# Quantised activations turned by a transposing DMA instead of TensorE, and gate matmuls ahead of up matmuls, in a fused convolution and quantised FFN kernel

## The chip, the cores and the metric

One core of one Trainium2 chip. The metric is the device time of one launch in microseconds; lower is better. Times of the kernel before: three runs, 221.1, 221.6 and 222.94 us, median 221.6. One further execution was profiled.

## The reference

The input x is 64 x 32 x 512 (batch, head, position), float32. What is computed, with the parameters' set-up left out:

```
kernel = S4D kernel of 32 heads, 512 taps (exp, sin, cos of 64 modes a head)
u      = x masked to each batch row's length
y      = (causal convolution of u with kernel + D * u), masked again
beta   = mean |y| over the 512 positions
q      = clip(round(y * sqrt(7) / (beta + 1e-5)), -8, 7)          # int4 values
gate   = q @ ternary(w_gate).T,  up = q @ ternary(w_up).T          # 512 -> 1376
inter  = up * relu(gate)^2       (with the scales of q and of the weights)
inter  = clip(round(inter * 127 / (max|inter| + 1e-5)), -128, 127) # int8 values
out    = x + inter @ ternary(w_down).T (with scales)               # 1376 -> 512
```

## The kernel before, in words

The 64 x 32 rows of 512 are cut into T = 16 tiles of 128 rows (two heads by 64 batch rows). A prologue of some 42 us loads and quantises the three weight matrices and makes the convolution's taps, which go to a buffer in DRAM, `k_back`. Then the loop over tiles runs, software-pipelined over three tiles and written out by hand: each engine has its own `body(m, j, p, k)`, called for k = 0 to 16 (SyncE to 17), with m = k and p = k % 2, and engines meet at semaphores alone. Each engine works its list in order, so a wait holds all that is listed behind it. The work of one tile n:

- **SyncE** loads x into `x_in` (two halves), and from `k_back` the Toeplitz matrix `toep` of the tile's two heads (512 KB), both by `load_ahead(m + 3, ...)`, and later x again as `x_res`. Nearly every large transfer is issued from this queue. The order in body m is: the transposing DMA of tile m - 1's `inter_q` into `it_int` (L365, waits for `inter_quant`), the store of tile m - 2's output (L369), `load_ahead(m + 3)` (L294, L316), `x_res` of tile m (L374). `load_ahead` is called for k < 13 only.
- **TensorE** turns x (`xt`, L465), into `tr_act_ps`; multiplies by `toep` (`conv`, L475), 16 records a tile; turns the rounded y (`qt`, L488: four 128 x 128 transposes into `tr_dve_ps`); makes gate and up in three chunks of 416, 512 and 448 columns (`products`, L562 and L564, four matmuls of each to a chunk, gate and up alternating); and multiplies by the down weights (`down`, L600, 11 matmuls). Body m holds: products 0 and 1 of tile m, xt(m + 2), products 2, down(m - 1), qt(m + 1), conv(m + 2). Gate and up have two PSUM banks each, taken in turn, so chunk 2 uses those of chunk 0 and waits for `relu_done` and `inter_ready` of chunk 0.
- **ScalarE** copies x's transpose (L652), sums |y| (`y_sum`, L657), rounds y (`y_round`, L661), and makes relu (L693) and square (L696) of each gate chunk. In body m: chunk 0, y_sum(m + 1), chunk 1, y_round(m + 1), chunk 2, the copy of x(m + 2).
- **VectorE** masks conv's result into `y` (L960), makes the scales (`y_scale`, L966 to L970), clips q into `q_t` (`q_copy`, L974), makes `inter` from up and the squared relu (L1034) and its maxima (L1038), quantises it (L1089), casts `it_int` to `i_t` (L1058), and adds the residual (L1105). In body m, from 2 on: gated(0), the cast of tile m - 1, y_scale(m + 1), gated(1), gated(2), q_copy(m + 1), the maximum and scales, the quantise of tile m, o_sb of tile m - 1, y_mask(m + 2).

`y_round` adds the float 1.5 * 2^23, so that the low 16 bits of the float32 `y_r` hold the integer; `y_low` is that half seen as bfloat16, and the transpose moves its bits unchanged. `q_copy` reads them from PSUM as int16 and clips to -8 to 7.

Of the kernel before, what the change touches and what calls it, by code (L numbers as in the profile page):

```python
# [20 lines left out]
P = 128  # L21
# [17 lines left out]
def adaln_ffn(nc, x, length, log_dt, C, log_A_real, A_imag, Dskip,  # L39
# [21 lines left out]
    with ExitStack() as ctx:  # L61
# [85 lines left out]
        y = sb("y", [P, L])  # L147
        y_r = sb("y_r", [P, L])
        ysum = [sb(f"ysum{p}", [P, 1]) for p in range(2)]
# [18 lines left out]

        y_low = y_r[:].bitcast(BF16)[:, ::2]
        by_re, by_im = (inter[:, i * HG * JB:(i + 1) * HG * JB].rearrange("p (c k) -> p c k", c=2) for i in range(2))  # L170
# [47 lines left out]
        q_copied = sem("q_copied")  # L218
        gu_done = sem("gu_done")
        relu_done = sem("relu_done")  # L220
# [63 lines left out]
        def _(sp):  # L284
# [74 lines left out]
            def body(m, j, p, k):  # L359
                if k == 1:  # L360
                    turn_down(0)
                if 1 <= k < T:
                    sp.wait_ge(inter_quant, m)
                    wait(sp, it_dve_copied, m - 1)
                    sp.dma_start_transpose(it_int[:], inter_q[:]).then_inc(it_loaded, 16)  # L365
                if k >= 2:
                    sp.wait_ge(out_ready, m - 1)
                    for half in range(2):
                        sp.dma_start(in_dram(out, m - 2, half), o_sb[p][half_rows(half), :]).then_inc(stored[p], 16)  # L369
                if k < T - 3:  # L370
                    load_ahead(m + 3, 1 - p)
                if k is None or k < T:
                    for half in range(2):
                        sp.dma_start(x_res[p][half_rows(half), :], in_dram(x, m, half)).then_inc(res_loaded[p], 16)  # L374
                if k == 0:
                    turn_down(1)
# [62 lines left out]
        def _(pe):  # L439
# [40 lines left out]
            def qt(n):  # L480
# [6 lines left out]
                for i in range(KB):  # L487
                    mm = pe.transpose(q_bank(n)[:, i * P // 2:(i + 1) * P // 2].bitcast(BF16),  # L488
                                      y_low[:, i * P:(i + 1) * P], ident_bf[:])
                mm.then_inc(q_turned, 1)  # L490
# [61 lines left out]
            def products(m, p, c, k):  # L552
                c0, cn = CH[c]
                bank = (NC * p + c) % 2
                pe.wait_ge(q_copied, m + 1)
                if k == 0:
                    wait(pe, w_dve_copied, copies_before(c, COPY_DVE))
                    pe.wait_ge(w_act_copied, copies_before(c, COPY_ACT))
                wait(pe, relu_done, NC * m + c - 1)
                wait(pe, inter_ready, NC * m + c - 1)  # L560
                for i in range(KB):
                    pe.matmul(gate_ps[bank][:, 0:cn], q_t[p][:, i, :], gate_t[:, i, c0:c0 + cn],  # L562
                              start=(i == 0), stop=(i == KB - 1))
                    mm = pe.matmul(up_ps[bank][:, 0:cn], q_t[p][:, i, :], up_t[:, i, c0:c0 + cn],  # L564
                                   start=(i == 0), stop=(i == KB - 1))
                mm.then_inc(gu_done, 1)

# [36 lines left out]
            def body(m, j, p, k):  # L604
# [13 lines left out]
                if k >= 2:  # L618
                    down(m, k)
                if k < T - 1:  # L620
                    qt(m + 1)
                if k < T - 2:
# [8 lines left out]
        def _(act):  # L631
# [22 lines left out]
            def y_sum(n, p):  # L654
                act.wait_ge(y_masked, n + 1)
                wait(act, q_turned, n)
                nc.scalar.activation(y_r[:], y[:], ACT.Abs, accum_out=ysum[p][:]).then_inc(y_summed, 1)  # L657

            def y_round(n):
                act.wait_ge(yscale_ready, n + 1)  # L660
                nc.scalar.activation(y_r[:], y[:], ACT.Identity, bias=round_col[:],  # L661
                                     scale=yscale[:]).then_inc(y_rounded, 1)

# [23 lines left out]
            def body(m, j, p, k):  # L687
                def relu_square(c):
                    cn = CH[c][1]
                    bank = (NC * p + c) % 2  # L690
                    act.wait_ge(gu_done, NC * m + c + 1)
                    wait(act, inter_ready, NC * m + c - 1)
# [35 lines left out]
        def _(dve):  # L728
# [243 lines left out]
            def q_copy(n, p):  # L972
                dve.wait_ge(q_turned, n + 1)
                v.tensor_scalar(q_t[p][:].rearrange("p k t -> p (k t)"), q_bank(n)[:, 0:L // 2].bitcast(I16),  # L974
                                -8.0, 7.0, ALU.max, ALU.min).then_inc(q_copied, 1)

# [42 lines left out]
            def body(m, j, p, k):  # L1019
# [9 lines left out]
                def gated(c):  # L1029

                    c0, cn = CH[c]
                    bank = (NC * p + c) % 2
                    dve.wait_ge(g2_ready, NC * m + c + 1)
                    v.scalar_tensor_tensor(out=inter[:, c0:c0 + cn], in0=up_ps[bank][:, 0:cn],  # L1034
                                           scalar=gu_scale[p][:, 1:2], in1=g2[bank][:, 0:cn],
# [40 lines left out]
                if k < T:  # L1076
                    step(gated(2))
                if 1 <= k < T - 1:
                    q_copy(m + 1, 1 - p)
                if k is None or k < T:  # L1080
# [3 lines left out]
                    step(v.tensor_scalar(gam127[:], gamma[:], EPS, 1.0 / 127.0, ALU.add, ALU.mult))  # L1084
                    step(v.reciprocal(iscale[:], gam127[:]))
                    if k != T - 1:
                        if k >= 1:
# [56 lines left out]
```

## Time and profile before

| | before |
|---|---|
| runs, us | 221.1, 221.6, 222.94 (median 221.6) |
| profiled execution, us | 221.94 |
| its span, us | 220.1 |
| granted TensorE clock, mean | 0.997 |
| TensorE matmul busy | 182.1 us, 83% |
| VectorE busy | 168.0 us, 76% |
| ScalarE busy | 115.2 us, 52% |
| GpSimd busy | 9.6 us, 4% |
| DMA queue of SyncE | 63.3% of 16 engines' time, 36.40 MB |

The span is what the profile's clock covers, from the first to the last instruction; the execution's own time has 1.8 us more around it. Busy time is the sum of what an engine's instructions take; TensorE's records overlap, because a matmul's record runs on while the next has started, so the distance from start to start tells what one costs. A name such as `g` or `ysum` in a row is a tile with its buffer number left out. In a row of the timeline, what stands in brackets at the end is the idle time before it and what ended it.

### The profile page before, as it was taken

How to read it: one execution, taken by the hardware profiler on the slowest of the kernel's cores; microseconds unless marked ns; L12 is line 12 of the kernel's file. 1: busy time of each engine (PE TensorE's matmuls, PEld its weight loads, DVE VectorE, ACT ScalarE, POOL GpSimd, SP SyncE). 2: the span in 40 equal slices, each digit the busy share in tenths (PEclk: the TensorE clock that was granted, in tenths of full speed). 3: DMA queues.
4: the chain of work that ended last, by engine and by line, in shares of the span. 5: the costliest groups of instructions: out<-in, count | busy, mean ns of one | idle time of the engine just before them, and what ended most of it. 6: DMA issues, size and time to landing. Idle time of an engine off the chain costs nothing.

```text
span 220.1 us, 3405 instructions
## 1 busy us (share of the span) xinstructions
PE 182.1 (83%) x1139; PEld 94.2 (43%) x1139; DVE 168.0 (76%) x457; ACT 115.2 (52%) x182; POOL 9.6 (4%) x27
## 2 busy tenths in 40 slices
PE   1010499699859899999999999999999999997882
PEld 1010296454324345455454545444545545443340
DVE  6999677769839687787878787878678787878671
ACT  2365976599812528273554546382827364553610
POOL 4043500000000000000000000000000000000000
PEclk9999999999999999999999999999999999999998
DMA  3999049992994929485856657584949475251613
GB/s 77 386 378 284 5 108 339 300 264 55 209 224 89 231 84 230 107 232 101 223 113 195 136 169 164 143 208 111 224 111 244 89 227 111 60 121 43 150 30 76
DMA packets 43824, 36.61 MB, mean 166 GB/s; under 512 B 30240, under 2 KB 30304, under 8 KB 43808
## 3 DMA queue, kind: packets, MB, share of 16 engines
q1 hardware_dynamic: 43488, 36.40, 63.3%
q8 instruction: 9, 0.15, 0.3%
q0 software_dynamic: 256, 0.00, 0.1%
q14 instruction: 7, 0.06, 0.1%
q10 hardware_dynamic: 64, 0.00, 0.0%
HBM read 25.27 MB, written 4.28 MB: 134 GB/s over the span
## 4 chain that ended last, share of the span: by engine, by line
PE 54%; DVE 3%; issue 3%; DMA 2%; ACT 1%; DVEq 0%
PE down_ps L600 14%; PE gate_ps L562 13%; PE up_ps L564 12%; PE conv_ps L475 12%; PE tr_act_ps L465 2%; DMA it_int<-inter_q 2%; PE tr_dve_ps L488 1%; PE conv_ps L519 1%; DVE inter L1034 1%; ACT g L693 1%; ACT g L696 1%; DVE i_t L1058 0%; DVE inter_q L1089 0%; ACT i_t L709 0%; DVE o_sb L1105 0%
## 5 line engine op out<-in xcount | busy, mean ns | idle before, releaser
L562 PE MATMUL gate_ps<-gate_t,q_t 128*128 128x416 bf16 (+2 forms) x192 | 68.6, 357 | 3.3 <-DVE q_t L974 2.1
L564 PE MATMUL up_ps<-up_t,q_t 128*128 128x416 bf16 (+2 forms) x192 | 68.5, 357 | 0.0
L693 ACT ACTIVATE g<-gate_ps,gu_scale 128x416 f32<-128x416 f32 (+2 forms) x48 | 30.3, 631 | 65.5 <-issue 50.4
L1034 DVE SCALAR_TENSOR_TENSOR inter<-up_ps,gu_scale,g 128x416 f32<-128x416 f32 (+2 forms) x48 | 33.2, 692 | 24.1 <-ACT g L696 24.1
L600 PE MATMUL down_ps<-down_t,i_t 128*128 128x512 bf16 (+1 forms) x176 | 40.7, 379 | 3.5 <-DVE down_t L955 1.9
L475 PE MATMUL conv_ps<-toep,x_t 128*64 128x512 f32 (+3 forms) x256 | 38.0, 439 | 1.6 <-ACT x_t L652 1.5
L1038 DVE TENSOR_REDUCE imax<-inter 128x1 f32<-128x416 f32 (+2 forms) x48 | 30.3, 631 | 1.7
L562 PEld LDWEIGHTS gate_ps<-gate_t,q_t 128*128 128x128 bf16 x192 | 18.7, 97 | 25.2 <-issue 7.3
L696 ACT ACTIVATE g<-g 128x416 f32<-128x416 f32 (+2 forms) x48 | 28.1, 585 | 1.5
L600 PEld LDWEIGHTS down_ps<-down_t,i_t 128*128 128x128 bf16 (+1 forms) x176 | 16.9, 98 | 23.9 <-DVE i_t L1058 4.0
L475 PEld LDWEIGHTS conv_ps<-toep,x_t 128*64 128x64 f32 x256 | 17.0, 136 | 21.2 <-issue 15.6
L564 PEld LDWEIGHTS up_ps<-up_t,q_t 128*128 128x128 bf16 x192 | 18.8, 98 | 15.0
L457 PE MATMUL down_ps<-wsum,averaging 128*128 128x1 f32 x12 | 2.6, 324 | 19.2 <-ACT int_gate L634 10.4
L661 ACT ACTIVATE y_r<-y,round_col,yscale 128x512 f32<-128x512 f32 x16 | 13.0, 813 | 10.3 <-DVE yscale L970 10.1
L1089 DVE TENSOR_SCALAR inter_q<-inter,iscale 128x1376 int16<-128x1376 f32 x15 | 14.0, 936 | 0.5
L1105 DVE SCALAR_TENSOR_TENSOR o_sb<-down_ps,oscale,x_res 128x512 f32<-128x512 f32 x16 | 11.9, 746 | 2.6 <-PE down_ps L600 2.6
L1058 DVE CAST i_t<-it_int 128x1408 bf16<-128x1408 int16 x15 | 7.8, 520 | 6.5 <-DMA it_int<-inter_q 6.5
L960 DVE SCALAR_TENSOR_TENSOR y<-steps,lens,conv_ps 128x512 f32<-128x512 f32 x16 | 11.8, 740 | 1.1 <-PE conv_ps L475 1.1
L657 ACT ACTIVATE y_r<-y 128x512 f32<-128x512 f32 x16 | 9.8, 614 | 2.4 <-DVE y L960 2.4
L457 PEld LDWEIGHTS down_ps<-wsum,averaging 128*128 128x128 f32 x12 | 2.4, 279 | 19.9 <-ACT int_gate L634 10.5
L465 PE MATMUL tr_act_ps<-ident,x_in 128*128 128x128 f32 x64 | 9.7, 275 | 0.0
L652 ACT COPY x_t<-tr_act_ps 128x512 f32<-128x512 f32 x16 | 9.1, 568 | 1.0 <-PE tr_act_ps L465 1.0
(169 smaller groups left out, 165.6 us busy)
## 6 DMA issues: line engine op xcount, KB each, us to landing
toep<-k_back SPq DMA_DIRECT2D x16, 512.0 KB, 4.9
x_in<-in_x_dram SPq DMA_DIRECT2D x32, 128.0 KB, 3.1
x_res<-in_x_dram SPq DMA_DIRECT2D x32, 128.0 KB, 4.0
out_dram<-o_sb SPq DMA_DIRECT2D x32, 128.0 KB, 2.6
raw_down<-in_L_ffn_w_down_dram SPq DMA_DIRECT2D x2, 1376.0 KB, 8.8
raw_gate<-in_L_ffn_w_gate_dram SPq DMA_DIRECT2D x1, 1536.0 KB, 7.0
raw_up<-in_L_ffn_w_up_dram SPq DMA_DIRECT2D x1, 1536.0 KB, 14.2
raw_gate<-in_L_ffn_w_gate_dram SPq DMA_DIRECT2D x1, 1024.0 KB, 9.3
```

The lines of the kernel that those rows point to most:

```text
L465: mm = pe.transpose(tr_act_ps[:, i * P:(i + 1) * P], x_in[p][:, i * P:(i + 1) * P], ident[:])
L475: mm = pe.matmul(conv_ps[half * B:(half + 1) * B, 0:L - i * P], x_t[:, i, half * B:(half + 1) * B], toep[p][:, half, i * P:L], start=(i == ...
L562: pe.matmul(gate_ps[bank][:, 0:cn], q_t[p][:, i, :], gate_t[:, i, c0:c0 + cn], start=(i == 0), stop=(i == KB - 1))
L564: mm = pe.matmul(up_ps[bank][:, 0:cn], q_t[p][:, i, :], up_t[:, i, c0:c0 + cn], start=(i == 0), stop=(i == KB - 1))
L600: mm = pe.matmul(down_ps[:], i_t[0:r, c, :], down_t[0:r, c, :], start=(c == 0), stop=(c == IB - 1))
L661: nc.scalar.activation(y_r[:], y[:], ACT.Identity, bias=round_col[:], scale=yscale[:]).then_inc(y_rounded, 1)
L693: nc.scalar.activation(g2[bank][:, 0:cn], gate_ps[bank][:, 0:cn], ACT.Relu, scale=gu_scale[p][:, 0:1]).then_inc(relu_done, 1)
L696: nc.scalar.activation(g2[bank][:, 0:cn], g2[bank][:, 0:cn], ACT.Square).then_inc(g2_ready, 1)
L1034: v.scalar_tensor_tensor(out=inter[:, c0:c0 + cn], in0=up_ps[bank][:, 0:cn], scalar=gu_scale[p][:, 1:2], in1=g2[bank][:, 0:cn], op0=ALU.mu ...
L1038: return v.tensor_reduce(imax[:, c:c + 1], inter[:, c0:c0 + cn], AX.X, ALU.max, apply_absolute_value=True)
L1089: v.tensor_scalar(inter_q[:, 0:I], inter[:], iscale[:], None, ALU.mult).then_inc(inter_quant, 1)
L1105: v.scalar_tensor_tensor(out=o_sb[1 - p][:], in0=down_ps[:], scalar=oscale[1 - p][:], in1=x_res[1 - p][:], op0=ALU.mult, op1=ALU.add).then ...
```

## The change

From tile 2 on, q is no longer turned on TensorE. `y_round` writes int16 directly into `y_i` (the sum of |y| now writes into a bfloat16 tile `y_abs`), SyncE issues a transposing DMA from `y_i` to `q_int` in bodies 1 to 14, between `load_ahead` and `x_res`, and `q_copy` reads `q_int` from SBUF. On VectorE `q_copy` moves from ahead of the maximum to between the reciprocal `iscale` and the quantise. Tiles 0 and 1 are still turned on TensorE. In `products` the four gate matmuls of a chunk come first, with a semaphore of their own (`gate_done`), then the wait for `inter_ready`, then the four up matmuls (`up_done`); relu waits for `gate_done` alone and the product on VectorE for `up_done` too.

```diff
@@ -145,7 +145,9 @@
         toep = [sb(f"toep{p}", [P, 2, L]) for p in range(2)]
         x_t = sb("x_t", [P, KB, P])
         y = sb("y", [P, L])
-        y_r = sb("y_r", [P, L])
+        y_abs = sb("y_abs", [P, L], BF16)
+        y_i = sb("y_i", [P, L], I16)
+        q_int = sb("q_int", [P, KB, P], I16)
         ysum = [sb(f"ysum{p}", [P, 1]) for p in range(2)]
         ybe = sb("ybe", [P, 1])
         yinv = sb("yinv", [P, 1])
...
@@ -369,6 +372,10 @@
                         sp.dma_start(in_dram(out, m - 2, half), o_sb[p][half_rows(half), :]).then_inc(stored[p], 16)
                 if k < T - 3:
                     load_ahead(m + 3, 1 - p)
+                if 1 <= k < T - 1:
+                    sp.wait_ge(y_rounded, m + 2)
+                    sp.wait_ge(q_copied, m + 1)
+                    sp.dma_start_transpose(q_int[:], y_i[:]).then_inc(q_loaded, 16)
                 if k is None or k < T:
                     for half in range(2):
                         sp.dma_start(x_res[p][half_rows(half), :], in_dram(x, m, half)).then_inc(res_loaded[p], 16)
...
@@ -486,7 +493,7 @@
                 wait(pe, q_copied, n)
                 for i in range(KB):
                     mm = pe.transpose(q_bank(n)[:, i * P // 2:(i + 1) * P // 2].bitcast(BF16),
-                                      y_low[:, i * P:(i + 1) * P], ident_bf[:])
+                                      y_i[:, i * P:(i + 1) * P].bitcast(BF16), ident_bf[:])
                 mm.then_inc(q_turned, 1)
 
             def copied(k):
...
@@ -557,13 +564,15 @@
                     wait(pe, w_dve_copied, copies_before(c, COPY_DVE))
                     pe.wait_ge(w_act_copied, copies_before(c, COPY_ACT))
                 wait(pe, relu_done, NC * m + c - 1)
+                for i in range(KB):
+                    mm = pe.matmul(gate_ps[bank][:, 0:cn], q_t[p][:, i, :], gate_t[:, i, c0:c0 + cn],
+                                   start=(i == 0), stop=(i == KB - 1))
+                mm.then_inc(gate_done, 1)
                 wait(pe, inter_ready, NC * m + c - 1)
                 for i in range(KB):
-                    pe.matmul(gate_ps[bank][:, 0:cn], q_t[p][:, i, :], gate_t[:, i, c0:c0 + cn],
-                              start=(i == 0), stop=(i == KB - 1))
                     mm = pe.matmul(up_ps[bank][:, 0:cn], q_t[p][:, i, :], up_t[:, i, c0:c0 + cn],
                                    start=(i == 0), stop=(i == KB - 1))
-                mm.then_inc(gu_done, 1)
+                mm.then_inc(up_done, 1)
 
             def turn_last():
 
...
@@ -617,8 +626,8 @@
                     turn_last()
                 if k >= 2:
                     down(m, k)
-                if k < T - 1:
-                    qt(m + 1)
+                if k == 0:
+                    qt(1)
                 if k < T - 2:
                     conv(m + 2, j + 1, p)
                 if k == 1:
...
@@ -653,13 +662,15 @@
 
             def y_sum(n, p):
                 act.wait_ge(y_masked, n + 1)
-                wait(act, q_turned, n)
-                nc.scalar.activation(y_r[:], y[:], ACT.Abs, accum_out=ysum[p][:]).then_inc(y_summed, 1)
+                nc.scalar.activation(y_abs[:], y[:], ACT.Abs, accum_out=ysum[p][:]).then_inc(y_summed, 1)
 
             def y_round(n):
                 act.wait_ge(yscale_ready, n + 1)
-                nc.scalar.activation(y_r[:], y[:], ACT.Identity, bias=round_col[:],
-                                     scale=yscale[:]).then_inc(y_rounded, 1)
+                if 1 <= n <= 2:
+                    act.wait_ge(q_turned, n)
+                if n >= 3:
+                    act.wait_ge(q_loaded, 16 * (n - 2))
+                nc.scalar.activation(y_i[:], y[:], ACT.Copy, scale=yscale[:]).then_inc(y_rounded, 1)
 
             for g in range(2):
                 act.dma_start(ldt_in[:, g:g + 1],
...
@@ -688,7 +699,7 @@
                 def relu_square(c):
                     cn = CH[c][1]
                     bank = (NC * p + c) % 2
-                    act.wait_ge(gu_done, NC * m + c + 1)
+                    act.wait_ge(gate_done, NC * m + c + 1)
                     wait(act, inter_ready, NC * m + c - 1)
                     nc.scalar.activation(g2[bank][:, 0:cn], gate_ps[bank][:, 0:cn], ACT.Relu,
                                          scale=gu_scale[p][:, 0:1]).then_inc(relu_done, 1)
...
@@ -970,9 +981,14 @@
                 v.tensor_scalar(yscale[:], yinv[:], SQRT7, None, ALU.mult).then_inc(yscale_ready, 1)
 
             def q_copy(n, p):
-                dve.wait_ge(q_turned, n + 1)
-                v.tensor_scalar(q_t[p][:].rearrange("p k t -> p (k t)"), q_bank(n)[:, 0:L // 2].bitcast(I16),
-                                -8.0, 7.0, ALU.max, ALU.min).then_inc(q_copied, 1)
+                dst = q_t[p][:].rearrange("p k t -> p (k t)")
+                if n < 2:
+                    dve.wait_ge(q_turned, n + 1)
+                    src = q_bank(n)[:, 0:L // 2].bitcast(I16)
+                else:
+                    dve.wait_ge(q_loaded, 16 * (n - 1))
+                    src = q_int[:].rearrange("p k t -> p (k t)")
+                v.tensor_scalar(dst, src, -8.0, 7.0, ALU.max, ALU.min).then_inc(q_copied, 1)
 
             def k_copy(i):
 
...
@@ -1031,6 +1047,7 @@
                     c0, cn = CH[c]
                     bank = (NC * p + c) % 2
                     dve.wait_ge(g2_ready, NC * m + c + 1)
+                    dve.wait_ge(up_done, NC * m + c + 1)
                     v.scalar_tensor_tensor(out=inter[:, c0:c0 + cn], in0=up_ps[bank][:, 0:cn],
                                            scalar=gu_scale[p][:, 1:2], in1=g2[bank][:, 0:cn],
                                            op0=ALU.mult, op1=ALU.mult).then_inc(inter_ready, 1)
...
@@ -1075,14 +1092,14 @@
                     weight_round(2, 1)
                 if k < T:
                     step(gated(2))
-                if 1 <= k < T - 1:
-                    q_copy(m + 1, 1 - p)
                 if k is None or k < T:
 
                     step(v.tensor_reduce(gamma[:], imax[:], AX.X, ALU.max))
                     v.tensor_scalar(oscale[p][:], gamma[:], wscale_dn[:], None, ALU.mult)
                     step(v.tensor_scalar(gam127[:], gamma[:], EPS, 1.0 / 127.0, ALU.add, ALU.mult))
                     step(v.reciprocal(iscale[:], gam127[:]))
+                    if 1 <= k < T - 1:
+                        q_copy(m + 1, 1 - p)
                     if k != T - 1:
                         if k >= 1:
                             dve.wait_ge(it_loaded, 16 * m)
```

## Rows read from the trace of the kernel before

**Rows 1.** Waits of 85 to 187 us: total, times, longest.
```profile
PEld gate_ps L562 <- issue: 3.9, 20, 0.2
```

**Rows 2.** Timeline of TensorE over one tile: start, us, instruction, [idle before].
```profile
124.40 0.60 PE L465 MATMUL tr_act_ps<-ident,x_in 128*128 128x128 f32 x4
125.01 0.35 PE L562 MATMUL gate_ps<-gate_t,q_t 128*128 128x448 bf16 x1
...
126.52 2.54 PE L600 MATMUL down_ps<-down_t,i_t 128*128 128x512 bf16 x11
128.90 0.39 PE L488 MATMUL tr_dve_ps<-ident_bf,y_r 128*128 128x128 bf16 x4
129.22 2.37 PE L475 MATMUL conv_ps<-toep,x_t 128*64 128x512 f32 x16
131.53 0.35 PE L562 MATMUL gate_ps<-gate_t,q_t 128*128 128x416 bf16 x1
```

**Rows 3.** Timeline of TensorE in the last tile but one.
```profile
196.88 0.35 PE L562 MATMUL gate_ps<-gate_t,q_t 128*128 128x448 bf16 x1 [0.45 <-DVE inter L1034]
```

**Rows 4.** Timeline of TensorE in the first tile.
```profile
48.60 0.64 PE L465 MATMUL tr_act_ps<-ident,x_in 128*128 128x128 f32 x4
49.07 0.35 PE L562 MATMUL gate_ps<-gate_t,q_t 128*128 128x448 bf16 x1
```

**Rows 5.** Timeline of VectorE and ScalarE over the same tile as rows 2.
```profile
124.22 0.65 DVE L1034 SCALAR_TENSOR_TENSOR inter<-up_ps,gu_scale,g 128x416 f32<-128x416 f32 x1 [1.26 <-ACT g L696]
...
125.41 0.52 DVE L1058 CAST i_t<-it_int 128x1408 bf16<-128x1408 int16 x1
...
126.60 0.81 ACT L661 ACTIVATE y_r<-y,round_col,yscale 128x512 f32<-128x512 f32 x1 [0.63 <-DVE yscale L970]
...
127.32 0.61 ACT L693 ACTIVATE g<-gate_ps,gu_scale 128x448 f32<-128x448 f32 x1
...
129.94 0.42 DVE L974 TENSOR_SCALAR q_t<-tr_dve_ps 128x512 bf16<-128x512 int16 x1
...
130.97 0.94 DVE L1089 TENSOR_SCALAR inter_q<-inter,iscale 128x1376 int16<-128x1376 f32 x1
```

**Rows 6.** Timeline of SyncE's queue over the same tile.
```profile
121.67 1.45 SPq L365 DMA_TRANSPOSE it_int<-inter_q  x1
123.17 1.39 SPq L369 DMA_DIRECT2D out_dram<-o_sb  x2
...
125.89 0.69 SPq L316 DMA_DIRECT2D toep<-k_back  x1
...
131.94 1.42 SPq L365 DMA_TRANSPOSE it_int<-inter_q  x1
```

**Rows 7.** The line of toep in 85 to 187 us: durations in ns, landings.
```profile
L316 SPq DMA_DIRECT2D toep<-k_back x10: 589/592/1535, 85.0 to 177.2; - x10
...
DMA to landing us min/median/max: 4.4/5.0/5.7
```

**Rows 8.** DMA issues of the whole span: us from issue to landing (median).
```profile
it_int<-inter_q SPq DMA_TRANSPOSE x15, 3.6
...
int_gate<-int_down SPq DMA_TRANSPOSE x2, 5.4
```

**Rows 9.** Stretches of one tile; last two columns: DMA share, GB/s.
```profile
121.50:122.50 1.00, 1.00 (x7) 0.54 (x6) 1.00 (x3) 0.00 (x0) 0.00 (x0) 1.00 0.00 0
123.00:124.50 1.50, 1.50 (x9) 0.73 (x7) 0.28 (x1) 1.47 (x3) 0.00 (x0) 1.00 1.11 212
...
127.50:129.50 2.00, 2.00 (x14) 1.00 (x13) 1.33 (x3) 1.48 (x3) 0.00 (x0) 1.00 0.94 297
```

**Rows 10.** SyncE's queue around the first changed tiles.
```profile
63.36 0.59 SPq L316 DMA_DIRECT2D toep<-k_back  x1
...
70.03 1.41 SPq L365 DMA_TRANSPOSE it_int<-inter_q  x1
```

**Rows 11.** The line of the it_int transpose in 85 to 187 us.
```profile
L365 SPq DMA_TRANSPOSE it_int<-inter_q x10: 1300/1411/1449, 90.9 to 183.3; - x10
```

More of the change, by code:

```diff
@@ L166, in adaln_ffn @@
         o_sb = [sb(f"o_sb{p}", [P, L]) for p in range(2)]
-        y_low = y_r[:].bitcast(BF16)[:, ::2]
         by_re, by_im = (inter[:, i * HG * JB:(i + 1) * HG * JB].rearrange("p (c k) -> p c k", c=2) for i in range(2))
@@ L218, in adaln_ffn @@
         q_copied = sem("q_copied")
-        gu_done = sem("gu_done")
+        q_loaded = sem("q_loaded")
+        gate_done = sem("gate_done")
+        up_done = sem("up_done")
         relu_done = sem("relu_done")
```

## The prediction

> **What bounds the kernel now.** I read the waits first, then the timeline of one tile on each engine, then the landings of the transfers. In the steady stretch TensorE has no wait of its own in the view of waits; all that it shows at a chunk's first matmul is a weight load that comes 0.2 us late, 20 times for ten tiles [rows 1]. The timeline of a tile shows why the period is what it is: the first gate matmul of the next tile starts at 131.53, and the queue of SyncE repeats after 131.94 - 121.67 = 10.27 us [rows 2, 6]. Two items of that are not products. The four transposes of q hold TensorE from 128.90 to 129.22, 0.32 us. The gap from the input transposes to chunk 2 is 125.01 - 124.40 = 0.61 us, where the first tile, with nothing to wait for, needs 49.07 - 48.60 = 0.47 [rows 2, 4]. The other 0.14 is a wait for VectorE: chunk 2 shares its banks with chunk 0, and the product that frees them ends at 124.22 + 0.65 = 124.87 [rows 5]; where no input transpose lies between, the same wait shows in full, 0.45 us [rows 3]. So TensorE is the bound, and 0.46 us of its tile could go.
>
> A second ring is nearly as long, and the reader must see it before believing that gain. It goes from the transpose of inter_q (issued 121.67) to its landing 3.6 us later [rows 6, 8], the cast into i_t at 125.41, the y scale, y_round at 126.60, the relu of chunk 2 behind it at 127.32, the product, the maximum, q_copy at 129.94, the quantise at 130.97, and the next issue at 131.94 [rows 5, 6]. The landing is at 125.27 and the cast at 125.41, so the slack is at most 0.14 us: this ring needs 10.13.
>
> The third view is the queue of DMAs. SyncE issues, in this order and without pause, the transpose (A), the output 1.50 us later, x_in, toep at A + 4.22, x_res [rows 6]. The engines are idle before A's packets arrive, then run at 212 GB/s and a share of 1.11 without change from 123.0 to 124.5, though the output was issued at 123.17, and the rest follows (297 GB/s at 127.5 to 129.5) [rows 9]. What is issued on this queue is served in order, then. toep lands a median 5.0 us (4.4 to 5.7) after its issue [rows 7], at A + 9.2, only about 1 us before the next A.
>
> **The change part by part.** Off TensorE: from tile 2 on 0.32 us of q transposes go. Whether the 0.09 or so between the last of them and conv (four at about 0.06 make 0.23) is theirs or conv's own start can't be told; 0.23 to 0.32 goes. The 0.14 of chunk 2 goes as well: its gate matmuls now wait only for relu(0), and the four of them cover the wait for the product, which now guards the up matmuls alone. TensorE would need 10.27 - 0.14 - (0.23 to 0.32) = 9.81 to 9.90 us. The regrouped order costs nothing else: each matmul had its own weight load before and has it still. relu(0) is released four matmuls (some 0.7 us) earlier, but the ring above starts at the cast, which waits for the transfer; that gain is hidden.
>
> ScalarE: y_round writes int16 and has no bias tile. Rows give 0.81 us for it now; nothing shows the new form, which I put at 0.61 (the relu of 448 columns) to 0.81, no change taken. Its new wait for the q of the tile before, and the lost wait of y_sum for q_turned, are long satisfied.
>
> VectorE: q_copy reads int16 from SBUF in place of PSUM, 0.42 us now. The cast of 1408 columns takes 0.52 [rows 5], so 512 columns take between 512/1408 of that, 0.19, and 0.42; I take 0.3, of which 0.25 passes before the quantise can start. What matters is its new place: ahead of the quantise, on an engine that works in order. **Its wait for q_loaded now holds the quantise, its output transpose, the o_sb product and y_mask, and through them everything that SyncE issues next.**
>
> SyncE: the new issue stands behind toep. It waits for y_rounded, which comes at 126.60 + 0.81 = 127.41, A + 5.74; x_res behind it has a whole tile of time, and the wait for q_copied is old. So it is issued some 1.2 us later than the queue would allow, and what then counts is when the transfer lands.
>
> **The landing of q.** The trace has no 512-column transpose. The one of 1408 columns lands in 3.6 us, the one of 2816 in 5.4 [rows 8]: 1.8 us per 1408 columns, so 0.65 us of transfer for 512 and 1.8 before and after it. On an empty queue it would land 2.45 us after its issue, at A + 8.2. But the queue isn't empty: 512 KB of toep are ahead of it and land at A + 9.2, and in order it can't land before them. So q lands at A + 4.22 + 5.0 + 0.65 = A + 9.87 (9.27 to 10.57 with the ends of toep). Then 0.05 until VectorE starts, 0.25 of q_copy, and 130.97 to 131.94, 0.97, from the quantise to the next issue: the ring is **9.87 + 0.05 + 0.25 + 0.97 = 11.14 us**, against 10.27. Everything in it is measured from A, so a longer tile doesn't give the queue time to drain; TensorE waits some 1.2 us per tile at q_copied instead of bounding it.
>
> The Trainium skill bears on this from two sides. "DMA: Bandwidth & Descriptors", Queues, rings and completion order, says that each DMA engine takes descriptors in ring order and that the completion lands after everything earlier on that engine; the rates above agree. The same page, Anatomy of one DMA, fits 2.0 us plus bytes over 436 GB/s for a transfer (on GpSimd's path): an estimate of 2.3 us for these 128 KB, by which q would land at A + 8.0 and the first rival below would hold; for toep the same fit gives 3.2 us, where the trace has 5.0, and the measurement decides.
>
> **The sum.** The issues of the inter_q transpose from tile 2's body (70.03) to tile 13's (183.28) are 11 periods, 113.25 us [rows 10, 11]; at 11.14 they take 122.5, +9.3. The first q by DMA (body 1) lands at 63.36 + 5.0 + 0.65 = 69.0, and 1.27 later, at 70.3, comes the issue that was at 70.03 [rows 10]: +0.3. From body 13 on no toep is loaded, so q is in time there: two periods at about 10.06 (next paragraph), -0.4, and the 0.45 us wait in rows 3 partly gone, -0.2. Together +9.0 on the profiled execution's 221.94 (span 220.1), which stands 0.34 above the median of 221.6: 230.6 us on the scale of the median.
>
> **Rivals.** *Hidden transfer, faster.* If q isn't held by toep (served beside it, or toep lands sooner once x_res is issued after it), it lands before the maxima are done, at about A + 8.9, and the second ring bounds: 10.13 less 0.12 to 0.17 for the shorter q_copy, less 0 to 0.2 if y_round shrinks, 9.8 to 10.0 us. 13 periods save 3.5 to 6, the last tiles 0.5: 216 to 218, say 217.5. For it: the empty-queue price of 2.45 us. Against it: the order of service in rows 9. Chance 0.17. *Short tail of toep.* toep lands in 4.4 always, since nothing reads HBM behind it: ring 10.54, +2.6 for 11 periods, +0.3 - 0.6: 224. Chance 0.13. *Transfer dearer.* If the transpose can't start until the last engine has finished toep and then pays part of its start again (1.8 us less what overlaps, say 0.6), the ring is 11.74: +15.9 - 0.3, 237. Chance 0.08. *The regrouping undoes itself* (up matmuls wait for the product and the 0.14 stays): less than 2 us, inside the other cases; 0.02 for that with a hidden transfer, no change.
>
> **How the numbers follow.** Forecast 0.60: 230.6 us, with 227 to 234 for it alone. One per cent is about what a measurement of this kernel can tell from no change. Faster by over 1%: the hidden transfer, 0.17. Within 1% (219.4 to 223.8): the undoing and the low part of the short tail, 0.08. Slower: 0.75. The range reaches from within the short tail to the dearer transfer, 222 to 237.
>
> **What would show it.** Right: the q transpose issued about 5.8 us after the one of inter_q and landing at least 3.5 us after its own issue, behind toep; idle time of VectorE at q_copy put down to that DMA; TensorE idle 1 us or more at L562's place; ScalarE's first relu of a tile starting while the up matmuls of chunk 0 still run. Period 11.1 with toep, about 10.0 without. Wrong: a landing within 2.5 us of the issue, a period under 10.1, and TensorE without a gap. The weakest step is that a transpose queued behind toep adds its 0.65 us and no more to toep's last landing; and it would also be wrong if toep's 5.0 us hangs on what is behind it.

## The result, and the profile after

The changed kernel is slower: 228.14 us median against 222.03 us of the kernel before in the same session, ratio 1.0285 with an interval of 1.0217 to 1.0353. The profiled execution took 230.12 us, the longest of its runs; the others lie between 227.49 and 228.23. Ratios leave out an execution more than 1.5% longer than the fastest of its kernel, and the profiled executions of two kernels below (with a dash in the table) are such ones, so that of their rows only the landing of q is read. A ratio isn't exactly the quotient of the medians.

The page of the changed kernel, its span, busy time of the engines and the chain that ended last by engine:

```profile
span 228.3 us, 3326 instructions
...
PE 179.1 (78%) x1083; PEld 90.8 (40%) x1083; DVE 167.3 (73%) x457; ACT 114.5 (50%) x182; POOL 9.4 (4%) x27
...
DMA 31%; DVE 13%; PE 7%; ACT 4%; SPq 2%; issue 2%; DVEq 0%
```

TensorE has less to do than before (179.1 us of busy time against 182.1), and the chain has left it: in the kernel before TensorE's part of the chain was 54% of the span, now it is 7%, and 31% is DMA, half of that each for the transpose of inter_q and the one of y. TensorE's clock isn't the cause: from 70 us to 192 us the granted clock is 1.00, and in the run with the transposing DMA alone, as slow as this one, its mean is 1.000. The waits say who stands still for them (total, times, longest):

```profile
DVE i_t L1075 <- DMA it_int<-inter_q: 15.8, 15, 4.3
...
DVE q_t L991 <- DMA q_int<-y_i: 12.3, 9, 2.1
PE gate_ps L568 <- DVE q_t L991: 11.9, 11, 2.3
```

VectorE waits at q_copy, for the new transfer; TensorE waits at the first gate matmul of a tile, for q_copy. One tile, where the kernel before has [rows 5, 6] (line numbers have moved: L368 is the transpose of inter_q, L319 toep, L378 the new transpose, L991 q_copy, L1106 the quantise):

```profile
125.02 1.40 SPq L368 DMA_TRANSPOSE it_int<-inter_q  x1
...
128.58 0.53 DVE L1075 CAST i_t<-it_int 128x1408 bf16<-128x1408 int16 x1 [0.87 <-DMA it_int<-inter_q]
...
129.24 0.59 SPq L319 DMA_DIRECT2D toep<-k_back  x1
...
129.78 0.72 ACT L673 ACTIVATE y_i<-y,yscale 128x512 int16<-128x512 f32 x1 [1.48 <-DVE yscale L981]
130.41 0.61 ACT L704 ACTIVATE g<-gate_ps,gu_scale 128x448 f32<-128x448 f32 x1
...
130.53 1.21 SPq L378 DMA_TRANSPOSE q_int<-y_i  x1
...
133.54 0.16 DVE L1100 RECIPROCAL iscale<-gam 128x1 f32<-128x1 f32 x1
...
134.97 0.29 DVE L991 TENSOR_SCALAR q_t<-q_int 128x512 bf16<-128x512 int16 x1 [1.26 <-DMA q_int<-y_i]
135.17 0.93 DVE L1106 TENSOR_SCALAR inter_q<-inter,iscale 128x1376 int16<-128x1376 f32 x1
...
135.31 0.88 PE L568 MATMUL gate_ps<-gate_t,q_t 128*128 128x416 bf16 x4 [0.78 <-DVE q_t L991]
...
136.13 1.43 SPq L368 DMA_TRANSPOSE it_int<-inter_q  x1
```

Read it from A = 125.02. toep is issued at A + 4.22 as before. y_round ends at 130.50 and q's transpose is issued at once, at A + 5.51. The scale that the quantise needs is ready at 133.70. The quantise starts at 135.17 all the same, because q_copy stands ahead of it and waits 1.26 us for q. The next issue is at 136.13: 11.11 us after A, where the tile in [rows 6] took 10.27. Landings in us after the issue, medians from 60 to 212 us, beside [rows 7, 8]:

```profile
toep<-k_back SPq DMA_DIRECT2D x12, 512.0 KB, 4.6
...
it_int<-inter_q SPq DMA_TRANSPOSE x15, 3.5
q_int<-y_i SPq DMA_TRANSPOSE x14, 4.2
```

In this tile toep lands 4.9 us after its issue, at 134.1. q lands 4.34 us after its own issue, as the chain has it:

```profile
130.53 4.34 DMA q_int<-y_i
```

That is 134.87, some 0.7 us behind toep, though q was issued 3.6 us before toep's landing. In the bodies without a toep load the same transpose lands in 2.5 us:

```profile
q_int<-y_i SPq DMA_TRANSPOSE x1, 2.5
```

The issues of the inter_q transpose from tile 2's body to tile 13's, beside [rows 10, 11]:

```profile
70.99 1.38 SPq L368 DMA_TRANSPOSE it_int<-inter_q  x1
...
191.98 2.00 SPq L368 DMA_TRANSPOSE it_int<-inter_q  x1
```

These 11 tiles take 120.99 us against 113.25.

### The profile page after: what moved, and what is told of

Same layout as the page of the kernel before. It is cut to its first block, busy times and chain, and to the rows that moved or that the text cites. A ratio compares the mean times of both kernels' runs of the same rounds, so it can differ in the third digit from the quotient of the medians.

```text
span 228.3 us, 3326 instructions
## 1 busy us (share of the span) xinstructions
PE 179.1 (78%) x1083; PEld 90.8 (40%) x1083; DVE 167.3 (73%) x457; ACT 114.5 (50%) x182; POOL 9.4 (4%) x27
## 4 chain that ended last, share of the span: by engine, by line
DMA 31%; DVE 13%; PE 7%; ACT 4%; SPq 2%; issue 2%; DVEq 0%
DMA it_int<-inter_q 16%; DMA q_int<-y_i 15%; DVE inter_q L1106 4%; DVE i_t L1075 2%; PE down_ps L609 2%; ACT y_i L673 2%; DVE inter L1051 2%; SPq L297 2%; PE gate_ps L568 1%; PE up_ps L573 1%; PE conv_ps L482 1%; DVE imax L1055 1%; ACT g L704 1%; SPq L319 1%; ACT g L707 1%
## 5 line engine op out<-in xcount | busy, mean ns | idle before, releaser
L568 PE MATMUL gate_ps<-gate_t,q_t 128*128 128x416 bf16 (+2 forms) x192 | 45.2, 358 | 11.9 <-DVE q_t L991 11.9
L573 PE MATMUL up_ps<-up_t,q_t 128*128 128x416 bf16 (+2 forms) x192 | 45.0, 357 | 0.0
L482 PE MATMUL conv_ps<-toep,x_t 128*64 128x512 f32 (+3 forms) x256 | 39.7, 454 | 6.0 <-ACT x_t L661 5.9
L482 PEld LDWEIGHTS conv_ps<-toep,x_t 128*64 128x64 f32 x256 | 17.5, 140 | 31.4 <-issue 16.7
L568 PEld LDWEIGHTS gate_ps<-gate_t,q_t 128*128 128x128 bf16 x192 | 17.4, 98 | 28.2 <-DVE q_t L991 15.2
L673 ACT ACTIVATE y_i<-y,yscale 128x512 int16<-128x512 f32 x16 | 11.5, 721 | 19.6 <-DVE yscale L981 19.4
L1106 DVE TENSOR_SCALAR inter_q<-inter,iscale 128x1376 int16<-128x1376 f32 x15 | 14.0, 931 | 0.1
L991 DVE TENSOR_SCALAR q_t<-q_int 128x512 bf16<-128x512 int16 x14 | 4.1, 294 | 12.5 <-DMA q_int<-y_i 12.3
L665 ACT ACTIVATE y_abs<-y 128x512 bf16<-128x512 f32 x16 | 10.0, 624 | 3.0 <-DVE y L971 3.0
```

What stands on the lines that cost most here:

```text
L482: mm = pe.matmul(conv_ps[half * B:(half + 1) * B, 0:L - i * P], x_t[:, i, half * B:(half + 1) * B], toep[p][:, half, i * P:L], start=(i == ...
L568: mm = pe.matmul(gate_ps[bank][:, 0:cn], q_t[p][:, i, :], gate_t[:, i, c0:c0 + cn], start=(i == 0), stop=(i == KB - 1))
L673: nc.scalar.activation(y_i[:], y[:], ACT.Copy, scale=yscale[:]).then_inc(y_rounded, 1)
L1106: v.tensor_scalar(inter_q[:, 0:I], inter[:], iscale[:], None, ALU.mult).then_inc(inter_quant, 1)
```

## The experiments

Each was timed beside the kernel before on the same chip, but not all on one chip, so only ratios are compared between them. The table has the ratio with its interval; the median landing of q's transpose, from its issue; and the mean distance of the inter_q transposes in the profiled execution, from body 2 to body 15 (13 tiles). Profiled executions differ from the median of their kernel by up to 3 us, so the last column orders the kernels only roughly. The two last kernels leave out part of the work.

| run | ratio | landing, us | mean tile, us |
|---|---|---|---|
| before | 1 | | 10.29 |
| changed kernel | 1.0285 (1.0217 to 1.0353) | 4.2 | 10.85 |
| regrouped matmuls alone | 1.0013 (0.9976 to 1.0051) | | 10.37 |
| transposing DMA alone | 1.0248 (1.0186 to 1.0311) | 3.7 | 10.69 |
| transpose without a user | 1.0003 (0.9967 to 1.0039) | 3.9 | 10.31 |
| q ahead of toep | 0.9994 (0.9954 to 1.0033) | 2.5 | 10.13 |
| quantise first | 0.9958 (0.9915 to 1.0001) | 3.7 | - |
| both orders | 0.9924 (0.9894 to 0.9954) | 2.5 | - |
| both orders, alternating | 1.0268 (1.0207 to 1.0329) | 2.5 | 10.59 |
| q ahead of toep, alternating | 0.9921 (0.9889 to 0.9954) | 2.5 | 10.28 |
| half of toep | 0.9994 (0.9956 to 1.0033) | 3.2 | 10.21 |
| an eighth of toep | 0.9819 (0.9752 to 0.9887) | 2.6 | 9.97 |

**Regrouped matmuls alone.** The kernel before, with the new `products`, relu's wait and the product's wait.

```diff
+                for i in range(KB):
+                    mm = pe.matmul(gate_ps[bank]...)
+                mm.then_inc(gate_done, 1)
                 wait(pe, inter_ready, NC * m + c - 1)
                 for i in range(KB):
-                    pe.matmul(gate_ps[bank]...)
                     mm = pe.matmul(up_ps[bank]...)
```

> The kernel before with one part of the change alone: gate matmuls of a chunk ahead of its up matmuls; q stays on TensorE. Theory (TensorE's 0.14 us wait at chunk 2 was the only thing to gain, and the ring over the inter_q transpose then bounds at 10.13 us): period 10.27 falls to about 10.13, some 2 us in all, 219.5 to 220.5, ratio 0.991. Rival A (regrouping is worth nothing, the 0.14 us is not a wait): 221.6 to 222.4, period 10.27. Rival B (it is part of why the changed kernel is slower): above 223.

Ratio 1.0013: the expected 2 us don't show. The single tile does gain. In the one that starts at 131.68 chunk 2 follows the input transposes after 134.69 - 134.25 = 0.44 us, where [rows 2] have 0.61:

```profile
134.25 0.60 PE L466 MATMUL tr_act_ps<-ident,x_in 128*128 128x128 f32 x4
134.69 0.92 PE L562 MATMUL gate_ps<-gate_t,q_t 128*128 128x448 bf16 x4
```

SyncE's queue shows the shorter tile, and what took the gain away:

```profile
141.78 1.42 SPq L366 DMA_TRANSPOSE it_int<-inter_q  x1
...
151.91 1.42 SPq L366 DMA_TRANSPOSE it_int<-inter_q  x1
...
163.69 1.41 SPq L366 DMA_TRANSPOSE it_int<-inter_q  x1
```

The first of these tiles takes 10.13 us, as the ring over the inter_q transpose was said to allow; ten of the 13 tiles lie between 10.10 and 10.14. The next takes 11.78: that ring now has no slack (VectorE's cast waits 0.6 us for the transpose in the short tiles too), so a late landing of the transpose passes into the time in full. Its landings:

```profile
DMA to landing us min/median/max: 3.5/3.6/5.2
```

The latest is at 5.2 us, in the tile of 11.78; in the kernel before it was 4.2. Rival B falls. Rival A has the time right, but not its reason: the wait of 0.14 us was there, and is gone. Why some landings come late, and whether they always eat the gain, the runs don't settle.

**Transposing DMA alone.** The changed kernel with alternating matmuls.

> The changed kernel with gate and up matmuls alternating again: the transposing DMA alone. Theory (the changed kernel is bounded by the landing of q behind toep, 9.5 to 9.9 us after the issue of the inter_q transpose, and by nothing on TensorE): the same as the changed kernel, 227 to 229. Rival (the regrouping gains its 2 us beside it): 230 or more. Rival (the regrouping costs): 226 or less.

Ratio 1.0248, 227.56 us: the same as the changed kernel within the intervals. The loss is the DMA's part, and what the regrouping adds to it or takes from it is too small to be told (the intervals are 0.6% to either side).

**Transpose without a user.** The kernel before, with a transpose of the same size from a constant tile at the same place.

```diff
                     load_ahead(m + 3, 1 - p)
+                if 1 <= k < T - 1:
+                    sp.wait_ge(y_rounded, m + 2)
+                    if k > 1:
+                        sp.wait_ge(q_loaded, 16 * (k - 1))
+                    sp.dma_start_transpose(q_int[:], steps[:].bitcast(I16)[:, 0:L]).then_inc(q_loaded, 16)
```

> The kernel before with a transposing DMA of the same size and at the same place in SyncE's order, waiting for y_rounded, whose result nobody uses; q stays on TensorE, and nobody waits for the transfer but the next of its kind. Theory (the loss is in who waits for the transfer, not in the transfer): 221.5 to 223, ratio under 1.005; its landing is 4 us or more, as in the changed kernel. Rival (the load on the DMA engines and SyncE's wait slow the other transfers): the inter_q transpose lands later than 3.6 us, and 225 or more.

```profile
it_int<-inter_q SPq DMA_TRANSPOSE x15, 3.5
q_int<-steps SPq DMA_TRANSPOSE x14, 3.9
```

It lands in 3.9 us, nearly as late as in the changed kernel, the inter_q transpose lands as before, and the ratio is 1.0003. Within 0.4% the transfer costs nothing; waiting for it does.

**q ahead of toep.** The load of toep goes behind q's transpose in SyncE's body; with `late=True` `load_ahead` loads x_in alone.

```diff
-                    load_ahead(m + 3, 1 - p)
+                    load_ahead(m + 3, 1 - p, late=True)
                 if 1 <= k < T - 1:
                     ...
                     sp.dma_start_transpose(q_int[:], y_i[:]).then_inc(q_loaded, 16)
+                if k < T - 3:
+                    load_toep_ahead(m + 3, 1 - p)
```

> The changed kernel with SyncE's order changed: q's transpose ahead of the load of toep, which now waits for y_rounded too. Theory (q is late only because it stands behind 512 KB of toep): q lands about 2.5 us after its issue, VectorE no longer waits for it, the period falls to 9.9 to 10.4 (toep then reaches into the next inter_q transpose by up to 0.5 us), 217 to 222. Rival (a transposing DMA of y costs some 4 us wherever it stands): landing at 4 us, 226 to 229. Rival (toep, issued 1.3 to 3 us later, delays the inter_q transpose behind it by as much as q gained): q lands in 2.5 us, the inter_q transpose in 4.5 or more, 226 or more.

```profile
toep<-k_back SPq DMA_DIRECT2D x16, 512.0 KB, 4.7
...
it_int<-inter_q SPq DMA_TRANSPOSE x15, 3.7
q_int<-y_i SPq DMA_TRANSPOSE x14, 2.5
```

With 512 KB less ahead of it the same transpose lands in 2.5 us, and the loss is gone (0.9994). toep is used a tile later and has time. The issues at the start of the first and at the end of the last of the 13 tiles:

```profile
69.35 1.39 SPq L372 DMA_TRANSPOSE it_int<-inter_q  x1
...
200.99 1.26 SPq L372 DMA_TRANSPOSE it_int<-inter_q  x1
```

131.64 / 13 = 10.13 us a tile; the shortest are at 9.85, within what was put down as TensorE's own need, 9.81 to 9.90.

**Half and an eighth of toep.** From tile 4 on `load_toep` brings 256 or 64 of the 512 columns; the order is that of the changed kernel. The rest of toep is stale there, so both leave out part of the work. The edit with 64 columns:

```diff
+                if tile < 4:
                     ...
+                else:
+                    src = bass.AP(k_back, (2 * tile) * (L + P), [[1, P], [L + P, 2], [1, 64]])
+                    sp.dma_start(toep[p][:, :, 0:64], src).then_inc(toep_loaded[p], 16)
```

> The changed kernel with the load of toep cut to half (256 of 512 columns, 1 KB runs) from tile 4 on, the rest stale: part of the computation is left out. Theory (bytes ahead in the queue): the landing of q falls in proportion, 4.2 to about 3.3 us, between the changed kernel and the one with an eighth: period 9.9 to 10.4, 218 to 223. Rival (any load ahead of the transpose costs the same, by its completion and not by its bytes): q still lands in some 4 us, 226 or more.

> The changed kernel with the load of toep cut to an eighth (64 of 512 columns) from tile 4 on, so the rest of toep is stale there: part of the computation is left out. Theory (q waits for the bytes of toep ahead of it in the queue): q lands in 2.5 us in place of 4.2, VectorE stops waiting for it, period 9.9, 216 to 219. Rival (the transpose has a price of its own beside other transfers or on this queue): q lands in 3.5 us or more, 224 or more.

The two kernels, half first:

```profile
toep<-k_back SPq DMA_DIRECT2D x12, 256.0 KB, 3.8
...
q_int<-y_i SPq DMA_TRANSPOSE x14, 3.2
```

```profile
toep<-k_back SPq DMA_DIRECT2D x12, 64.0 KB, 2.9
...
q_int<-y_i SPq DMA_TRANSPOSE x14, 2.6
```

q's landing falls with the bytes ahead of it: 4.2, 3.2, 2.6 us for 512, 256 and 64 KB. So the price is the bytes ahead, not the completion of a load.

**q from ScalarE's queue.** From tile 3 on, behind y_round; one execution each, the second with an eighth of toep.

```diff
+                if n >= 3:
+                    act.wait_ge(y_rounded, n + 1)
+                    act.wait_ge(q_copied, n)
+                    act.dma_start_transpose(q_int[:], y_i[:]).then_inc(q_loaded, 16)
```

> The changed kernel with the transpose of q issued from ScalarE's queue, right behind y_round, from tile 3 on. It costs ScalarE some 1.2 us ahead of chunk 2's relu, which lies on the ring, so the time tells little: 225 to 231. What is asked is the landing. Theory (q is late by its place in SyncE's queue): on a queue of its own it lands in 2.5 to 3.5 us while toep is still going. Rival (the DMA engines serve in order of issue over both queues, or toep's load delays a transpose whatever its queue): 4 us or more.

> q's transpose from ScalarE's queue as in the run before, and the load of toep cut to an eighth from tile 4 on, the rest stale: part of the computation is left out. Theory (both queues share the 16 DMA engines, and a transpose ends only when every engine has done its share of what is on it): without toep's bytes it lands in 2.5 to 3.5 us from ScalarE's queue too. Rival (a transpose from ScalarE's queue is slow of itself): 4.5 us or more again.

The landing in the first and in the second kernel:

```profile
q_int<-y_i ACTq DMA_TRANSPOSE x13, 5.4
```

```profile
q_int<-y_i ACTq DMA_TRANSPOSE x13, 3.5
```

The first theory failed, and the second held at its edge. On a queue of its own q lands later, 5.4 us against 4.2, and takes 3.5 where only an eighth of toep is loaded, against 2.6 in SyncE's queue. toep's bytes delay it whichever queue it is on. The queue isn't slow of itself: in the last two bodies of the first kernel, where no toep is loaded and x_res is issued some 2 us ahead of q, the transpose lands in 2.5 us:

```profile
q_int<-y_i ACTq DMA_TRANSPOSE x2, 2.5
```

That x_res, which follows q on SyncE's queue, now runs beside it is a likely reason for the rest, but wasn't tried. The times, 250.43 and 243.82 us, are far above what I expected; the tile of the first shows one part of it, ScalarE's own issue ahead of chunk 2's relu:

```profile
124.81 0.72 ACT L673 ACTIVATE y_i<-y,yscale 128x512 int16<-128x512 f32 x1 [1.49 <-DVE yscale L985]
...
125.57 1.21 ACTq L677 DMA_TRANSPOSE q_int<-y_i  x1
126.88 0.64 ACT L708 ACTIVATE g<-gate_ps,gu_scale 128x448 f32<-128x448 f32 x1 [1.34 <-issue]
```

y_round ends at 125.53 and the relu starts at 126.88, 1.35 us later, where it followed at once before. The last two tiles of the first kernel, in which q is in time and ScalarE still issues, are 11.3 us long; in the others q's later landing comes on top.

**Quantise first.** The order of SyncE stays; on VectorE q_copy goes behind the quantise.

```diff
                     step(v.reciprocal(iscale[:], gam127[:]))
-                    if 1 <= k < T - 1:
-                        q_copy(m + 1, 1 - p)
                     if k != T - 1:
                         ...
                         v.tensor_scalar(inter_q[:, 0:I], inter[:], iscale[:], None, ALU.mult).then_inc(inter_quant, 1)
+                        if k >= 1:
+                            q_copy(m + 1, 1 - p)
```

> The changed kernel with q_copy put behind the quantise on VectorE instead of ahead of it; SyncE's order stays. q lands as late as in the changed kernel, but its wait no longer holds the quantise. Theory (the cost is the in-order wait, which ties the inter_q transpose to the landing of q; TensorE has about 0.5 us to spare): VectorE and TensorE may still wait at q, but the next inter_q transpose is issued on time, so waits don't add up: period 9.9 to 10.3, 217 to 222. Rival (the landing itself bounds, and the wait only moves to TensorE, whose next tile starts late): 226 to 229 with idle time of 1 us a tile at gate_ps.

Ratio 0.9958, with q as far back in the queue as in the changed kernel. It does land late, by the median as late as with the transposing DMA alone (3.7 us), which loses 2.5%:

```profile
q_int<-y_i SPq DMA_TRANSPOSE x14, 3.7
```

Moving one wait behind one instruction takes back all of the loss. So the late landing by itself doesn't bound; it did because the quantise, and with it everything SyncE issues next, was queued behind the wait for it.

**Both orders, and the matmuls' part in them.**

> The changed kernel with both orders altered: q's transpose ahead of toep's load on SyncE, and q_copy behind the quantise on VectorE. Theory (two separate losses, each alone brings the period to 9.9 to 10.1 with single tiles held by late landings): clean tiles at 9.85, TensorE's own need, and fewer long ones, since q has 1.5 us of slack: 218 to 220.5, ratio 0.985 to 0.993. Rival (what is left is the inter_q transpose's own late landings, which neither order touches): the same as either alone, 221.4 to 221.7.

Ratio 0.9924: some 1.7 us under the kernel before, at the upper edge of what was expected; the next kernel but one is level with it, and of the kernels that do all the work these two are the fastest. Its interval overlaps that of quantise first, so that the second order adds to the first isn't shown. Then the same with alternating matmuls:

> The kernel with both orders altered, but gate and up matmuls alternating again. Theory (its clean tiles are bounded by TensorE at 9.85 us, where chunk 2's wait of 0.14 us counts): the regrouping is worth 1 to 2 us there, so 222 to 223. Rival (the regrouping is worth nothing, here as in the kernel before): 220.5 to 221.5.

1.0268: the regrouping is worth 3.5% here (1.0268 over 0.9924), far more than the 1 to 2 us that the theory gave it. A tile of this kernel shows a ring that I had passed over (L371 is the inter_q transpose, L994 q_copy, L1077 the cast):

```profile
122.20 1.56 SPq L371 DMA_TRANSPOSE it_int<-inter_q  x1
...
122.43 0.35 PE L574 MATMUL gate_ps<-gate_t,q_t 128*128 128x416 bf16 x1 [0.37 <-DVE q_t L994]
...
124.09 0.61 ACT L707 ACTIVATE g<-gate_ps,gu_scale 128x416 f32<-128x416 f32 x1 [4.49 <-issue]
...
125.38 0.65 DVE L1053 SCALAR_TENSOR_TENSOR inter<-up_ps,gu_scale,g 128x416 f32<-128x416 f32 x1 [1.70 <-ACT g L710]
...
126.57 0.52 DVE L1077 CAST i_t<-it_int 128x1408 bf16<-128x1408 int16 x1
...
132.57 0.29 DVE L994 TENSOR_SCALAR q_t<-q_int 128x512 bf16<-128x512 int16 x1
132.68 1.68 SPq L371 DMA_TRANSPOSE it_int<-inter_q  x1
```

q_copy ends and chunk 0 starts at 122.43. Its relu comes at 124.09, only when all eight matmuls are done, the product at 125.38, the maximum of chunk 0 right after it, and the cast of i_t, which stands behind these on VectorE, at 126.57. From the cast on it is the known way over y_round, chunk 2 and the quantise to q_copy at 132.57; the issues are 132.68 - 122.20 = 10.48 us apart. With gate matmuls first the relu comes four matmuls earlier (0.97 us behind the start of chunk 0 in the changed kernel, 1.66 here), so the ring should be shorter by as much, by this estimate 9.8 us. It closes over the quantise only because q_copy stands behind it. That can be tried by leaving q_copy ahead:

> q's transpose ahead of toep's load, gate and up matmuls alternating, and q_copy ahead of the quantise as in the changed kernel: the run with both orders altered and alternating matmuls, less one of its two orders. That run was at 10.49 us a tile, by its trace on a ring from q_copy over chunk 0, its relu and product, the cast, y_round, chunk 2 and the quantise back to q_copy. Theory (that ring holds the quantise only because q_copy stands behind it, 0.85 us): here it is 9.6 us, the ring over the inter_q transpose bounds at about 10.1, 221 to 223.5. Rival (alternating matmuls cost their 0.5 us a tile wherever q comes by DMA in time): 10.4 or more, 226 to 229.

SyncE's issues of the inter_q transpose in this kernel:

```profile
111.11 1.48 SPq L371 DMA_TRANSPOSE it_int<-inter_q  x1
...
121.13 1.53 SPq L371 DMA_TRANSPOSE it_int<-inter_q  x1
```

10.02 us, ratio 0.9921: alternating matmuls cost nothing in this order (grouped ones, in q ahead of toep, are at 0.9994, which is no better). The ring is what held the other one: one instruction, q_copy, moved from behind the quantise to ahead of it, is worth 3.5% here, the other way round than in the changed kernel.

## Why the prediction was right

**What was right.** *What bounds before*: the regrouping alone, whose tiles fall from 10.27 to 10.1 us and no further, bears out the two nearly equal bounds, TensorE and the ring over the inter_q transpose (10.13 was said). *The step that decided*, that q lands behind toep and that its wait holds the quantise: landing 4.2 us, some 0.7 behind toep's (0.65 was estimated), 2.5 without toep in the queue (2.45 estimated). Both halves of the step were tested apart: taking toep from ahead and taking the quantise from behind each give back the whole loss. *The sequence* from q's landing to the next issue was put at 0.05 + 0.25 + 0.97 = 1.27; in the tile shown it is 136.13 - 134.87 = 1.26. *The small terms*: y_round takes 0.72 us (between 0.61 and 0.81), q_copy 0.29 (0.3 taken), and the regrouping is worth nothing that shows in the changed kernel. The signs named ahead came: q issued at A + 5.5 (5.8 was said), landing 3.5 us or more later in nine of the 11 tiles, VectorE idle at q_copy, TensorE idle ahead of the first gate matmul (0.78 us in the tile shown, 1.1 in the mean of 11), and the relu of chunk 0 at 125.17, while its up matmuls run.

**What was mis-sized.** The forecast was 9.0 us slower; 2.85% is 6.3. In the sum for the profiled execution the term of the 11 tiles was +9.3 and measured 120.99 - 113.25 = +7.7. The term that was mis-sized is the 5.0 us for toep's landing: in these 11 tiles it is 4.64 in the mean, between 3.7 and 5.8, which takes 4.0 us from the 11. The loss didn't shrink by as much, because SyncE issues toep late in two of them, 4.77 and 5.69 us after A in place of 4.22, which gives back 2.0; small terms give back 0.4 (q lands 0.67 us behind toep, not 0.65, and a tile with an early q stays at 9.9 us, because the other ring takes over). So the closeness of the mean tile, 11.0 against 11.14, is in part luck: two errors that offset each other. Why toep lands sooner stays open. That x_res isn't issued right behind it may be why, as toep also lands in 4.7 us in the mean with the transpose without a user, which holds x_res back in the same way; but with q ahead of toep x_res follows toep at once, and toep, issued later in the tile, lands in 4.7 as well. The term of the first changed tile, +0.3, was nothing: from body 1 to body 2 the issues are 9.65 us apart, as the 9.68 before. The two tiles without toep gave -0.5 (-0.4 forecast), the last part nothing (-0.2). The profiled execution was 1.0 us late before the change acts (its first inter_q transpose is at 61.34, before at 60.35; ScalarE's longest wait for a weight load is 7.2 us against 6.1); 7.7 + 1.0 - 0.5 is the 8.2 between the spans. The medians lie only 6.1 apart, so the terms of this execution overstate the loss of a typical one by some 2 us; the late start is 1.0 of that, and where the rest lies, one profile of each kernel can't tell.

**A premise that was too strong.** The prediction says that what is issued on this queue is served in order, and that q therefore can't land before toep. q didn't: it landed 0.54 to 0.73 us behind toep in all 11 tiles. But the rule itself doesn't hold for every transfer of the queue, by the trace of the kernel before. In the tile of [rows 6] toep is issued at 125.89 and the first half of x_res at 126.62:

```profile
toep<-k_back SPq DMA_DIRECT2D x1, 512.0 KB, 5.6
...
x_res<-in_x_dram SPq DMA_DIRECT2D x1, 128.0 KB, 3.8
```

So toep lands at 131.5 and the half of x_res, issued behind it, at 130.4; it is ahead of toep in 7 of the 11 tiles. What differs between that transfer and q's transpose no run tries, so that q would stay behind toep was right, and not assured by the premise.

**The rivals.** The hidden transfer, at 0.17, is what its own condition gives: where q isn't held by toep, tiles from 9.85 us come, 10.13 on average, where it said 9.8 to 10.0. But its time, 216 to 218, was too good: it took every tile for a clean one, and with q ahead of toep the ratio is 0.9994. Only the kernel with an eighth of toep, which leaves out part of the work, comes to it (0.9819, which is 217.6 on 221.6). The short tail of toep was half right, since toep did land sooner, though at 4.64 and not at 4.4. The dearer transfer didn't occur. The regrouping undoing itself has the time of the regrouping alone right, but falls by its trace: the 0.14 us wait is gone there.

**A reason that was wrong.** The prediction says that the earlier relu of chunk 0 is hidden behind the cast's transfer. That fits the kernel before and the changed one, where no gain shows, but it is no property of the regrouping: once q's transpose is ahead of toep and q_copy behind the quantise it is worth 3.5%.

## What to carry to other kernels

A transfer takes its price from its place in the queue and from who is queued behind the wait for it; look at both before its own bytes. Where an instruction must wait for a late transfer on an engine that works in order, try it behind the work that starts the next transfer of the loop: here one instruction moved so was worth 3%. But follow what hangs on that instruction first. Where q came in time and the matmuls alternated, the same place cost 3.5%, because chunk 0, and through it the next quantise, waits for q_copy. And when two rings of a loop are within 0.2 us of each other, take no gain from shortening one until the trace shows what late landings do to the other.

## What the runs showed of the hardware beyond this

- A transposing DMA from SBUF to SBUF on a free queue lands in a median 2.5 us for 128 x 512 int16 and in 3.5 to 3.6 for 128 x 1408, and its issue holds the issuing queue for 1.2 and 1.4 us.
- On another engine's queue it isn't served ahead of loads that are under way: 5.4 us from ScalarE's queue, 4.2 behind the same load in SyncE's, and 2.5 from either in the bodies without a load of toep.
- Landings on one queue needn't come in the order of issue: a 128 KB load issued 0.7 us behind one of 512 KB landed some 1 us ahead of it.
